# Two stores of rows summed on chip, issued without waiting for the accumulating transfers in DRAM

## Chip, cores and metric

The kernel runs on one core of one Trainium2 chip. The metric is the device time of one execution in microseconds (us). Each core has five engines that work side by side (TensorE, VectorE, ScalarE, GpSimd and SyncE, in the profile PE, DVE, ACT, POOL and SP) and 16 DMA engines, which all of its queues share: SP's queue (q1 in the profile), ACT's (q10) and GpSimd's (q0, whose transfers are made by software).

## What is computed

The input is x of shape (4, 256, 32, 32), that is 4096 tokens of 256 channels. Three blocks follow each other:

```python
x = gamma * attention_along_the_last_axis(x) + x
t = to_tokens(x)
t = t + norm(t) @ W1 + (memory @ norm(t)) @ W2 + bias
u = norm(t)
sel_val, sel_idx = top_k(sigmoid(u @ expert_sel.T), 2)
...
h = relu(einsum('td,edh->teh', u, keys))
out = einsum('teh,te,ehv->tv', h, w, values)
t = t + out
```

Each token goes to 2 of 32 experts, each with 64 hidden values. The last line is what the change concerns: the result of a token is the sum of two rows, one for each of its experts. The row of the first expert also carries the token's own value t.

## The kernel before

The work is cut into 32 tiles of 128 tokens. A first stage computes attention, the memory step, the norm and the routing of each tile, and GpSimd scatters two rows of each token, one for each expert, to a list in DRAM that is sorted by expert. Then comes the expert stage: 20 groups (`GROUPS`) of 4 slots of 128 rows. For each group SP loads the rows, TensorE transposes and multiplies them, VectorE weights the result and adds it (`weighted`, L1161), and GpSimd scatters every row with an indirect transfer to the output (`send_group`, L612 to L620). The tensor `out` has 2N = 8192 rows of 1 KB: the first expert's result of token i goes to row i, the second's to row N + i. Only rows 0 to N - 1 are read by the host in the end, so the second half must be added to the first. This is the drain, which starts when the last scatter has landed, and it does that for two sets of rows in two ways:

- **Rows 0 to 3327** (`IN_PLACE`, L47) are added in DRAM. GpSimd waits for all scatters (L628, L629) and issues four transfers (`SUMS`, L44) from the second half of `out` to the first that add to what they write (L632); each counts the semaphore `stored` up by 16.
- **Rows 3328 to 4095**, the tail (`TAIL_ROWS` = 6, L46), are added on chip. SP loads the tail of the first half (L448), ACT that of the second half (L843), each 768 KB as 128 partitions of 1536 numbers. VectorE adds them in two halves (L1203, `tail_added`), and SP stores the one half (L451) and ACT the other (L846), 384 KB each. Both count up `tail_stored`.

The two sets of rows have no row in common. The engines run independent programs in the order written; a wait holds up the instructions behind it on the same engine alone. In this kernel SP waits for `stored` (L450) ahead of its store, and ACT has a wait for the same value (L845) ahead of its own. At the end SP waits for both stores (L452, `tail_stored` at 32). No other engine waits for `stored` or `tail_stored`. The block ends when all engines are through (L69 in the trace stands for this end of each engine's program).

Of the kernel before, what the change touches and what calls it, by code (L numbers as in the profile page):

```python
# [43 lines left out]
SUMS = 4  # L44
# [21 lines left out]
def attention_moe(nc, x_cm, x_tok, wqk4, bqk4, wvT, bv, gamma, w1, w2, bias, selT, keys, values, out):  # L66
    slots_d = nc.dram_tensor("slot_rows", [NE * CAP + P, ROW], F32, kind="Internal").ap()

    with ExitStack() as ctx:  # L69
# [6 lines left out]
        def sem(name):  # L76
            return ctx.enter_context(nc.semaphore(name))
# [194 lines left out]
        stored = sem("stored")  # L272
# [28 lines left out]
        def tail_rows(r):  # L301

            return out[r * N + IN_PLACE:(r + 1) * N, :].rearrange("(p k) e -> p (k e)", k=TAIL_ROWS)

        def tail_half(i):
            return slice(i * TAIL_ROWS * C // 2, (i + 1) * TAIL_ROWS * C // 2)
# [68 lines left out]
        def _(sp):  # L375
# [71 lines left out]
                sp.wait_ge(y_sent[i], sent_before(GROUPS))  # L447
            sp.dma_start(tail[:, 0], tail_rows(0)).then_inc(ld_tail[0], 16)  # L448
            sp.wait_ge(tail_added, 1)
            sp.wait_ge(stored, 16 * SUMS)  # L450
            sp.dma_start(tail_rows(0)[:, tail_half(0)], tail[:, 0, tail_half(0)]).then_inc(tail_stored, 16)  # L451
            sp.wait_ge(tail_stored, 32)  # L452

        @block.gpsimd
        def _(pool):
# [179 lines left out]
        def _(act):  # L635
# [206 lines left out]
                act.wait_ge(y_sent[i], sent_before(GROUPS))  # L842
            a.dma_start(tail[:, 1], tail_rows(1)).then_inc(ld_tail[1], 16)  # L843
            act.wait_ge(tail_added, 2)
            act.wait_ge(stored, 16 * SUMS)  # L845
            a.dma_start(tail_rows(0)[:, tail_half(1)], tail[:, 0, tail_half(1)]).then_inc(tail_stored, 16)  # L846

        @block.vector
# [685 lines left out]
```

## Time and profile before

| what | us |
|---|---|
| median of 3 runs | 490.43 |
| lowest and highest of them | 489.68, 490.91 |
| span of the profiled execution, first to last instruction | 449.5 |
| median less the span | 40.9 |
| last scatter of the expert stage issued | 420.72 |
| accumulating transfers issued | from 423.45 |
| stores of the tail issued | 445.3 |

The page gives the profiled execution by its span; its own device time is not given, so the 40.9 us around the span are the median of the runs less the span. Times within the profile count from the start of the span. To read it: look for the place of the change at the very end of the timeline, for what SP waits there, and for what the DMA engines do in that time. In the tables by stretch, the DMA share is the mean busy share of the 16 DMA engines; it can come out a little over 1 because a packet's recorded time begins before that of the packet ahead of it has ended.

### The profile page before, as it was taken

Reading aid. Unit: us, or ns where it says so; the run is one execution under the profiler, and the core shown is the slowest. Engines: PE = TensorE matmul, PEld = TensorE weight load, DVE = VectorE, ACT = ScalarE, POOL = GpSimd, SP = SyncE. Lnnn points to the kernel's source line nnn. Section 1 sums busy time; section 2 is a strip of 40 time slices with the busy share of each in tenths; the row PEclk is TensorE's granted clock in tenths of the full one; section 3 lists DMA queues with packets and bytes.
Section 4 is the critical chain, followed back from the end, with each engine's and each line's share of the span. In section 5 each row is a group of like instructions: output and inputs, shape, how many; then the busy total and the mean of one; then the engine's idle time right before and its main releaser. Section 6 shows DMA issues by size and latency. Waiting matters only on the chain.

```text
span 449.5 us, 10462 instructions
## 1 busy us (share of the span) xinstructions
PE 379.7 (84%) x3007; PEld 291.5 (65%) x3007; DVE 334.4 (74%) x1027; ACT 277.4 (62%) x819; POOL 295.9 (66%) x383
## 2 busy tenths in 40 slices
PE   8989999999999999999999998768799969881000
PEld 3756787876787877787878786525687768771000
DVE  1865788986998986898999995883699988894010
ACT  1243577766677775777778785826599879770000
POOL 6334456775777776777788888763667777777700
PEclk9999999999999999999999999968899989898555
DMA  7999310141121111131121111126888665531297
GB/s 207 365 203 190 103 43 25 51 151 37 52 93 49 48 49 50 49 96 49 37 71 49 62 38 71 61 72 199 255 260 249 180 188 175 157 104 40 85 242 186
DMA packets 31321, 52.73 MB, mean 117 GB/s; under 512 B 7036, under 2 KB 24334, under 8 KB 30765
## 3 DMA queue, kind: packets, MB, share of 16 engines
q1 hardware_dynamic: 23104, 29.48, 24.4%
q0 software_dynamic: 7872, 21.40, 15.0%
q10 hardware_dynamic: 288, 1.18, 0.7%
q8 instruction: 25, 0.41, 0.4%
q14 instruction: 32, 0.26, 0.2%
HBM read 31.56 MB, written 25.73 MB: 127 GB/s over the span
## 4 chain that ended last, share of the span: by engine, by line
PE 51%; DVE 19%; issue 9%; POOL 6%; DMA 6%; ACT 3%; DVEq 2%; SPq 1%; ACTq 0%; POOLq 0%
PE bank L1347 21%; PE bank L1309 9%; PE bank L1238 6%; PE bank L1330 4%; DVE rows L1180 3%; DVE vT L1166 3%; PE bank L1337 3%; DMA out<-vT,dest 3%; POOL out L617 3%; DVE vT L862 2%; DVE z_lo L872 2%; DMA xc_or_xin<-out 2%; POOL slot_rows L520 2%; DVE q_s L1149 1%; PE bank L1220 1%
## 5 line engine op out<-in xcount | busy, mean ns | idle before, releaser
L1347 PE MATMUL bank<-vT,prob 128*128 128x256 f32 x512 | 116.0, 380 | 1.7 <-POOL prob L543 1.7
L1347 PEld LDWEIGHTS bank<-vT,prob 128*128 128x128 f32 x512 | 94.9, 190 | 14.1 <-POOL prob L543 2.3
L617 POOL DMA_INDIRECT out<-vT,dest x80 | 79.6, 996 | 28.4 <-issue 14.9
L520 POOL DMA_INDIRECT slot_rows<-rows,slot x64 | 65.0, 1015 | 16.7 <-issue 15.1
L543 POOL TENSOR_TENSOR prob<-prob,ginv 128x1024 f32<-128x1024 f32 x32 | 61.3, 1914 | 21.0 <-DVE ginv L964 21.0
L514 POOL TENSOR_TENSOR rstd<-rstd,half_neg 128x1 f32<-128x1 f32 x64 | 35.9, 561 | 46.9 <-ACT rstd L667 46.5
L726 ACT ACTIVATE prob<-prob 128x1024 f32<-128x1024 f32 x32 | 33.8, 1057 | 19.6 <-DVE prob L932 19.6
L928 DVE TENSOR_REDUCE gmax<-X 128x32 f32<-128x1024 f32 x32 | 39.2, 1224 | 7.9 <-PE X L1272 7.8
L958 DVE TENSOR_REDUCE gsum<-prob 128x32 f32<-128x1024 f32 x32 | 38.7, 1210 | 3.6 <-ACT prob L726 3.5
L932 DVE TENSOR_TENSOR prob<-X,gmax 128x1024 f32<-128x1024 f32 x32 | 39.2, 1224 | 1.1
L1166 DVE SCALAR_TENSOR_TENSOR vT<-bank,wgt,vT 128x256 f32<-128x256 f32 x80 | 33.2, 477 | 6.7 <-PE bank L1485 5.3
L1180 DVE COPY rows<-values_s 64x256 f32 x112 | 34.4, 307 | 3.6 <-issue 2.4
L1238 PE MATMUL bank<-wv,xc_or_xin 128*128 128x256 f32 x128 | 32.6, 384 | 2.4 <-DVE t L880 2.4
L663 ACT ACTIVATE squares<-t,mv 128x256 f32<-128x256 f32 x64 | 31.7, 495 | 2.2 <-DVE t L880 2.1
L862 DVE SCALAR_TENSOR_TENSOR vT<-bank,gam,gbv 128x256 f32<-128x256 f32 x32 | 14.9, 479 | 24.4 <-PE bank L1238 24.3
L822 ACT ACTIVATE k_s<-keys_s 128x128 f32 x112 | 24.7, 306 | 9.4 <-issue 9.3
L1238 PEld LDWEIGHTS bank<-wv,xc_or_xin 128*128 128x128 f32 x128 | 23.5, 189 | 9.1 <-DVE t L880 3.8
L703 ACT ACTIVATE rows<-t,rstd 128x256 f32<-128x256 f32 x32 | 19.2, 599 | 16.0 <-POOL rstd L516 16.0
L800 ACT ACTIVATE prob<-X 128x512 f32<-128x512 f32 x40 | 21.5, 590 | 11.3 <-PE X L1454 11.2
L807 ACT ACTIVATE vT<-xc_or_xin 128x256 f32<-128x256 f32 x48 | 24.8, 593 | 5.1 <-DMA out<-vT,dest 5.1
L1309 PE MATMUL bank<-w_hi,uT_hi 128*128 128x512 f32 x60 | 26.4, 440 | 0.1
L1466 PE MATMUL X<-prob,k_s 128*128 128x256 f32 x96 | 24.4, 400 | 0.7 <-ACT prob L800 0.7
(205 smaller groups left out, 851.6 us busy)
## 6 DMA issues: line engine op xcount, KB each, us to landing
xc_or_xin<-slot_rows SPq DMA_DIRECT2D x32, 130.0 KB
xt<-x_tok SPq DMA_DIRECT2D x32, 128.0 KB, 2.1
values_s<-values SPq DMA_DIRECT2D x2, 2048.0 KB, 28.5
out<-out POOLq DMA_DIRECT2D x4, 832.0 KB, 14.9
xc_or_xin<-x_cm SPq DMA_DIRECT2D x3, 1024.0 KB, 9.2
t<-slot_rows SPq DMA_DIRECT2D x16, 130.0 KB
t<-slot_rows SPq DMA_DIRECT2D x32, 65.0 KB
xc_or_xin<-slot_rows SPq DMA_DIRECT2D x32, 65.0 KB
```

The source lines that it names most:

```text
L514: g.tensor_tensor(rstd[:, t % 2, 1:2], rstd[:, t % 2, 0:1], half_neg[:, :], ALU.pow).then_inc(rstd_done, 1)
L520: g.indirect_dma_start(out=slots_d, out_offset=bass.IndirectOffsetOnAxis(ap=slot[:, t % RB, r:r + 1], axis=0), in_=rows[:, t % RB, r, :], ...
L543: g.tensor_tensor(prob[:, t % 2], prob[:, t % 2], ginv[:, t % 2].unsqueeze(2).to_broadcast([P, WT * KB, W]), ALU.mult).then_inc(prob_done, 1)
L617: g.indirect_dma_start(out=out, out_offset=bass.IndirectOffsetOnAxis(ap=dest[:, n % (2 * NB), k:k + 1], axis=0), in_=yb[:, n % NB, k, :], ...
L928: v.tensor_reduce(gmax[:, s % 2].rearrange("p (w j) -> p w j", w=WT), E.rearrange("p w (j v) -> p w j v", v=W), AX.X, ALU.max).then_inc(ma ...
L932: v.tensor_tensor(prob[:, s % 2].rearrange("p (j w) v -> p w j v", w=WT), E.rearrange("p w (j v) -> p w j v", v=W), gmax[:, s % 2].rearran ...
L958: v.tensor_reduce(gsum[:, s % 2], prob[:, s % 2], AX.X, ALU.add).then_inc(sum_done, 1)
L1166: v.scalar_tensor_tensor(out=yb[:, n % NB, k, :], in0=Y_p[n % 2][k % 2][:, k // 2, :], scalar=wgt[:, n % (2 * NB), k:k + 1], in1=yb[:, n % ...
L1180: done = v.tensor_copy(into, values_s[side, bass.ds(expert[2 * k + r], 1), :].rearrange("p e n -> p (e n)"))
L1238: mm = m.matmul(dst, x, w, start=(i == 0), stop=(i == len(terms) - 1))
L1309: mm = m.matmul(hz_at(t), u[:, t % 2, a, :], w[:, a].rearrange("p s n -> p (s n)"), start=(i == 0), stop=(i == len(terms) - 1))
L1347: mm = m.matmul(av_p, pr[:, j, :], vT[:, b % 2, j, :], start=(j == 0), stop=(j == KB - 1))
```

## The change

The wait for `stored` leaves both places ahead of the stores. SP gets it back behind its wait for `tail_stored`, as the last instruction of its program; ACT has none any more.

```diff
--- before.py
+++ after.py
@@ -447,9 +447,9 @@
                 sp.wait_ge(y_sent[i], sent_before(GROUPS))
             sp.dma_start(tail[:, 0], tail_rows(0)).then_inc(ld_tail[0], 16)
             sp.wait_ge(tail_added, 1)
-            sp.wait_ge(stored, 16 * SUMS)
             sp.dma_start(tail_rows(0)[:, tail_half(0)], tail[:, 0, tail_half(0)]).then_inc(tail_stored, 16)
             sp.wait_ge(tail_stored, 32)
+            sp.wait_ge(stored, 16 * SUMS)
 
         @block.gpsimd
         def _(pool):
@@ -842,7 +842,6 @@
                 act.wait_ge(y_sent[i], sent_before(GROUPS))
             a.dma_start(tail[:, 1], tail_rows(1)).then_inc(ld_tail[1], 16)
             act.wait_ge(tail_added, 2)
-            act.wait_ge(stored, 16 * SUMS)
             a.dma_start(tail_rows(0)[:, tail_half(1)], tail[:, 0, tail_half(1)]).then_inc(tail_stored, 16)
 
         @block.vector
```

No instruction that does work is added, taken out or moved. The waits differ on SP and ACT alone. On SP, at the end of its program (each row is a transfer or the end of the program, in brackets the semaphores it waits for):

```order
 L439 DMA xc_or_xin<-slot_rows 64x260
 L448 DMA xc_or_xin<-out 128x1536 [waits y_sent2,y_sent3,y_sent1,y_sent0]
-L451 DMA out<-xc_or_xin 128x768 [waits stored,tail_added]
-L69 UNCONDITIONAL_BRANCH [waits tail_stored]
+L450 DMA out<-xc_or_xin 128x768 [waits tail_added]
+L69 UNCONDITIONAL_BRANCH [waits stored,tail_stored]
```

The store now waits for the sum alone, and the end of the program for both. On ACT, at the same place:

```order
 L807 ACTIVATE vT<-xc_or_xin 128x256 x3
 L843 DMA xc_or_xin<-out 128x1536 [waits y_sent2,y_sent3,y_sent1,y_sent0]
-L846 DMA out<-xc_or_xin 128x768 [waits stored,tail_added]
+L845 DMA out<-xc_or_xin 128x768 [waits tail_added]
 L69 UNCONDITIONAL_BRANCH
```

Here the wait is gone, and none comes behind it.

## Rows read from the trace of the kernel before

**Rows 1.** page, busy tenths and DMA traffic in 40 slices of 11.2 us

```profile
DMA  7999310141121111131121111126888665531297
GB/s 207 365 203 190 103 43 25 51 151 37 52 93 49 48 49 50 49 96 49 37 71 49 62 38 71 61 72 199 255 260 249 180 188 175 157 104 40 85 242 186
```

**Rows 2.** timeline from 415 us: start us, us, engine, line, transfer

```profile
422.89 0.34 SPq L448 DMA_DIRECT2D xc_or_xin<-out  x1
422.90 0.38 ACTq L843 DMA_DIRECT2D xc_or_xin<-out  x1
423.45 3.55 POOL L632 DMA_DIRECT2D out<-out  x4 [1.75 <-DMA out<-vT,dest]
430.76 1.83 DVE L1203 TENSOR_TENSOR xc_or_xin<-xc_or_xin 128x768 f32<-128x768 f32 x2 [21.27 <-DMA xc_or_xin<-out]
445.31 0.34 SPq L451 DMA_DIRECT2D out<-xc_or_xin  x1
445.33 0.38 ACTq L846 DMA_DIRECT2D out<-xc_or_xin  x1
```

**Rows 3.** waits of the SP queue from 423 us: us, times, longest

```profile
SPq L450 <- DMA out<-out: 22.0, 1, 22.0
SPq L69 <- DMA out<-xc_or_xin: 3.0, 1, 3.0
SPq L69 <- PEq L69: 0.6, 1, 0.6
```

**Rows 4.** source L632, the four accumulating transfers

```profile
DMA to landing us min/median/max: 9.8/14.9/20.1
```

**Rows 5.** windows of 1 us; the last two numbers are DMA share, GB/s

```profile
426.00:427.00 1.00, 0.00 (x0) 0.00 (x0) 0.00 (x0) 0.00 (x0) 1.00 (x2) 0.50 1.02 412
443.00:444.00 1.00, 0.00 (x0) 0.00 (x0) 0.00 (x0) 0.00 (x0) 0.00 (x0) 0.50 1.03 213
444.00:445.00 1.00, 0.00 (x0) 0.00 (x0) 0.00 (x0) 0.00 (x0) 0.00 (x0) 0.50 0.38 73
445.00:446.00 1.00, 0.00 (x0) 0.00 (x0) 0.00 (x0) 0.00 (x0) 0.00 (x0) 0.50 0.00 0
```

**Rows 6.** DMA queues, 428 to 430 us: packets, MB, share of the 16 engines

```profile
q0 software_dynamic: 48, 0.32, 77.3%
q10 hardware_dynamic: 37, 0.17, 21.9%
q1 hardware_dynamic: 26, 0.06, 8.8%
```

**Rows 7.** the same from 431 to 444 us, accumulation alone

```profile
DMA packets 464, 2.77 MB, mean 213 GB/s; under 512 B 48, under 2 KB 48, under 8 KB 464
...
q0 software_dynamic: 464, 2.77, 103.7%
```

**Rows 8.** the same with the issues (KB, us to landing) from 445.5 to 448.5 us, the stores alone

```profile
DMA packets 288, 0.79 MB, mean 262 GB/s; under 512 B 32, under 2 KB 32, under 8 KB 288
...
q10 hardware_dynamic: 144, 0.39, 33.6%
q1 hardware_dynamic: 144, 0.39, 32.7%
...
out<-xc_or_xin SPq DMA_DIRECT2D x1, 384.0 KB, 3.1
out<-xc_or_xin ACTq DMA_DIRECT2D x1, 384.0 KB, 3.3
```

**Rows 9.** windows at the end of the accumulation, same columns

```profile
444.30:444.60 0.30, 0.00 (x0) 0.00 (x0) 0.00 (x0) 0.00 (x0) 0.00 (x0) 0.50 0.16 22
444.60:444.70 0.10, 0.00 (x0) 0.00 (x0) 0.00 (x0) 0.00 (x0) 0.00 (x0) 0.50 0.03 0
444.70:445.30 0.60, 0.00 (x0) 0.00 (x0) 0.00 (x0) 0.00 (x0) 0.00 (x0) 0.50 0.01 0
```

## The prediction

> **What bounds the kernel now.** Only the drain can change, so I read the profile from its end. First the page's busy tenths [rows 1]: in the last three and a half slices TensorE's work is over and the DMA engines are at 9 tenths again; the reader is to see that the end of this kernel is a DMA stage. Then the timeline [rows 2]: the two tail loads are issued at 422.9, the four accumulating transfers from 423.45 on, VectorE adds the tail from 430.76 for 1.83 us, and then no engine does anything until 445.3, when both stores are issued, 12.7 us after the sum was ready. The waits of SP [rows 3] say for what: 22.0 us, up to 445.3, for the accumulation. Its last transfer landed 20.1 us after its issue [rows 4]; issued near 425.2, that is 445.3 too. So the chain of the end is: accumulation landed (445.3), SP issues its store (0.34 us), waits 3.0 us for both stores, which gives 448.65, and then 0.85 us go by until the span's end at 449.5, with 0.6 us of it in the closing barrier [rows 2, 3].
>
> The third view is the one that decides, the DMA share by stretch. From 443 to 444, with the accumulation alone, all 16 engines are taken (share 1.03, 213 GB/s), and the same holds for the 13 us from 431 to 444 (103.7%) [rows 5, 7]. There is no idle DMA time into which the stores could be put before 444.3 or so. Idle are the DMA engines only afterwards: the last packets of the accumulation end by 444.7, SP learns of it 0.6 us later, and from 445 to 446 nothing moves at all [rows 5, 9].
>
> **The change, part by part.**
>
> 1. *The wait ahead of the stores goes.* SP's store can be issued when the first half is added, 430.76 + 0.92 = 431.7, ACT's when the second is, at 432.6 [rows 2]. What leaves the path is the whole stretch from 445.3 to 448.65: 0.34 + 3.0 = **3.34 us**, if `stored` still arrives at 445.3. What is late next is `stored` itself.
>
> 2. *The stores' bytes now stand in the way of the accumulation.* Alone, the two stores took 33.6 + 32.7 = 66.3% of the 16 engines over 3.0 us, which is 1.99 us of every engine, with 256 data packets (288 less 32 small ones), 16 on each engine at 0.12 us [rows 8]. By bytes it is the same: 0.79 MB in 1.99 us are 397 GB/s. How much of it delays the accumulation the trace doesn't show directly, so I bound it. From below: nothing, if a store's packet could be moved beside an accumulating one, since the rate while accumulating is only 213 GB/s against the 412 of the loads alone [rows 5]. From above: I take twice the price, 4.0 us, as for engines that lose as much again at every turn between queues. The nearest row is the stretch from 428 to 430, in which the last tail loads ran beside the accumulation [rows 6]: 0.32 MB of accumulation are worth 0.32/0.213 = 1.50 us at its own rate, 0.17 + 0.06 = 0.23 MB of loads at 412 GB/s 0.56 us, together 2.06 us of work in 2 us. So the queues took turns and hid 3% of it. I take the full 1.99 us: `stored` is seen at 445.3 + 2.0 = 447.3.
>
>  What the slow rate means is a question on which the Trainium skill bears. The row: 213 GB/s of bytes written, 0.54 of the stores' rate [rows 7, 8]. The rule (Collectives: The Full Stack, "The bandwidth ceiling: the fold count and why AG ≠ RS ≠ AR"): an add in a DMA is slower not by its arithmetic but because it must read two sources over one read ring, which halves the rate. The trace's ratio of 0.54 agrees with it. By that rule the reading side is full, and a store, which must read too, is delayed in full, as I take it; if it were the adder that is slow, the sum would lean to the lower bound and save 3.3 us.
>
> 3. *In which order the packets go doesn't matter.* The accumulation has 32 data packets a microsecond, 2 on an engine, so 0.5 us each (464 less 48 small ones in 13 us) [rows 7]. One of each queue in turn makes 8 rounds of 0.5 + 2 x 0.12 us, 6 us, and the stores would land before 440. If they were served last of all, they would end with the accumulation at 444.6 + 2.0. The engines' work is the same sum, so the last landing stays near 447.3.
>
> 4. *The wait at SP's end.* Nothing is queued behind it but the closing barrier. ACT is through after its issue; VectorE, GpSimd and TensorE wait for neither semaphore. SP's other wait, for the stores, is over by then or ends with it. The 0.85 us behind the last landing stay.
>
> The sum: the span ends at 445.3 + 2.0 + 0.85 = 448.15 in place of 449.5, **1.35 us less** (3.34 - 1.99). Against the median, 40.9 us above the span, it is 490.43 - 1.35 = **489.1 us**, or 0.27%. A measurement of this kernel can tell about 0.3%, here 1.47 us, from no change, and its three runs spread over 1.2 us; the forecast lies just inside that bound.
>
> **The rivals.**
>
> *Part of the stores is hidden.* The loads of [rows 6] read DRAM as the accumulation does; the stores read the chip's own memory, which the accumulation never touches, and could fill gaps better than they did. If a third of the 1.99 us is hidden, the saving is 3.34 - 1.33 = 2.0 us, and the time 488.4; if all is, 487.1. For it: the shares above 1, which show packets overlapping. Against: 1.037 is the accumulation's share even alone [rows 7], so what overlap there is it has already. The Trainium skill would put the time near there too (DMA: Bandwidth & Descriptors, "Anatomy of one DMA — SWDGE (gpsimd) path": a fixed 2.0 us a transfer, mostly the confirmation of the last write, plus bytes over 436 GB/s): the fixed part would leave the path, 2.0 us, for 488.4. For the stores here the rows show 3.34 us less 1.99 us of moving, a fixed part of 1.35 us.
>
> *The turns cost something.* If the accumulating packets run longer beside the stores, say 0.1 us in each of 8 rounds, 0.8 us of the gain is lost, and the time is 489.9. [Rows 6] speak against it, though for loads only.
>
> *Slower: reads and writes collide in DRAM.* The loads only read DRAM; the stores write it, in the middle of an accumulation that reads and writes it as well. All gain is lost when the delay reaches 3.34 us, 1.35 more than the packets' own time: 0.17 us for each of the 8 accumulating packets of an engine that run beside a store, 0.50 to 0.67. To be slower by over 0.3% it takes 2.8 us more, 0.35 us each, for 491.9. Nothing in the trace looks like it: the rate is 213 GB/s in every stretch [rows 5, 7], whatever is being written.
>
> *The stores go early in name only.* Should their packets be held back until the accumulation is done, they would land 2.6 us after 444.6, near 447.2, and `stored` no later than 445.3: again about 1.4 us saved. The order of the landings would differ, the time hardly.
>
> **How the numbers follow.** The forecast, with a saving of 1.1 to 1.6 us however the packets are ordered, gets 0.62; a measurement puts about a third of that beyond 0.3% (0.20) and the rest within (0.42). Part hidden 0.24, all of it faster. Turns that cost something 0.11, within 0.3%. Slower 0.03. That makes 0.44 faster, 0.53 no difference, 0.03 slower. The range goes down to 488.0, a delay of 0.9 us by the stores, and up to 490.2, where the turns take nearly all of the gain; the ends beyond, 487.1 and 491.9, are left out.
>
> **What would show it.** Right: stores issued at 431.7 and 432.6 and landed near 440; from 432 to 439 a mixed rate above 213 GB/s with all engines taken; the last accumulating transfer landed about 2 us later than now, near 447.3; SP's last long wait for that transfer, and 0.85 us behind it. Wrong: a landing at 445.3 to 446.5 (stores hidden), or beyond 448.2 (turns or DRAM). If the drain is as I say and the time is not, it lies outside the span.

## The result, and the profile after

The change makes the kernel slower: a median of 491.47 us against 489.61 us, in 14 runs each, a ratio of 1.0044 with a 95% interval of 1.0026 to 1.0062, that is some 2.1 us by the ratio. The forecast was 489.1 us, 1.35 us less, with 0.03 for slower by over 0.3%.

One number of the prediction has to be put right first. Every later profile names the time of its own execution, and it is 1.7 to 2.2 us above its span: here 490.86 us for a span of 489.1 us. So the first profile of the kernel before, with its span of 449.5 us, was of an execution of some 451 us, 35 us below the fastest (486.24 us) of 43 timed runs of that kernel, in this comparison and the first one below (481.85 us is the lowest in the later ones); the "40.9 us around the span" are the difference of two unlike executions. The unchanged kernel profiled again (b_again) has a span of 488.9 us. The 40 us lie in the expert stage, as the rows of its scatters show, in the first trace and in b_again (durations in ns, first and last start in us):

```profile
L617 POOL DMA_INDIRECT out<-vT,dest x80: 978/981/1102, 314.9 to 420.7; - x80
```

```profile
L617 POOL DMA_INDIRECT out<-vT,dest x80: 978/980/988, 316.0 to 460.4; - x80
```

Its first scatter comes at nearly the same time, its last one 40 us later; why that one execution was faster stays open. The drain behind it is the same in both within 0.3 us, and traces are compared below by what follows the issue of the accumulation.

The end of the timeline after the change (start us, us, engine, line, transfer), against [rows 2]:

```profile
460.25 0.34 SPq L448 DMA_DIRECT2D xc_or_xin<-out  x1
460.26 0.38 ACTq L843 DMA_DIRECT2D xc_or_xin<-out  x1
460.82 3.55 POOL L632 DMA_DIRECT2D out<-out  x4 [1.75 <-DMA out<-vT,dest]
467.92 1.83 DVE L1202 TENSOR_TENSOR xc_or_xin<-xc_or_xin 128x768 f32<-128x768 f32 x2 [14.85 <-DMA xc_or_xin<-out]
468.90 0.34 SPq L450 DMA_DIRECT2D out<-xc_or_xin  x1
469.77 0.35 ACTq L845 DMA_DIRECT2D out<-xc_or_xin  x1
```

The waits of the SP queue behind that point (us, times, longest), against [rows 3]:

```profile
SPq L452 <- DMA out<-out: 15.7, 1, 15.7
SPq L450 <- DVE xc_or_xin L1202: 8.3, 1, 8.3
SPq L447 <- DMA out<-vT,dest: 5.1, 1, 5.1
SPq L69 <- PEq L69: 3.9, 1, 3.9
```

The issues' times to landing (KB, us), against [rows 4, 8]:

```profile
out<-out POOLq DMA_DIRECT2D x4, 832.0 KB, 16.7
...
out<-xc_or_xin SPq DMA_DIRECT2D x1, 384.0 KB, 10.2
out<-xc_or_xin ACTq DMA_DIRECT2D x1, 384.0 KB, 10.7
```

The stores do what the change says: issued at 468.9 and 469.8 and landed some 10 us later, at 479.1 and 480.5, they are through 4 us before the accumulation lands at 484.9. The 15.7 us at L452 begin when SP has issued its store, so they hold both waits, the one for the stores and the one for `stored`; the second ends last. The last row of the waits is the one that matters: in the closing barrier SP now waits 3.9 us where it waited 0.6 [rows 3]. The name of its releaser (PE's queue) is no help: TensorE's own end of program is over at 451.3 us, 34 us before SP comes to the barrier. Who is late there is shown by the rows of L69, which stands for the end of each engine's program (engine, operation, durations in ns, start). In the kernel before:

```profile
L69 PEldq DRAIN  x1: 2023/2023/2023, 405.7 to 405.7; - x1
L69 POOLq DRAIN  x1: 24492/24492/24492, 424.7 to 424.7; - x1
L69 DVEq DRAIN  x1: 1803/1803/1803, 430.8 to 430.8; - x1
L69 ACTq DRAIN  x1: 152/152/152, 445.7 to 445.7; - x1
...
L69 SPq DRAIN  x1: 7/7/7, 448.8 to 448.8; - x1
```

and after the change:

```profile
L69 PEldq DRAIN  x1: 3808/3808/3808, 447.5 to 447.5; - x1
L69 POOLq DRAIN  x1: 26777/26777/26777, 462.1 to 462.1; - x1
L69 DVEq DRAIN  x1: 1805/1805/1805, 468.0 to 468.0; - x1
L69 ACTq DRAIN  x1: 162/162/162, 470.2 to 470.2; - x1
...
L69 SPq DRAIN  x1: 7/7/7, 485.1 to 485.1; - x1
```

GpSimd ends its program with a DRAIN that starts as its last transfer is issued, so it looked like nothing but waiting for the accumulation. But it ends at 424.7 + 24.5 = 449.2 before, when the accumulation landed at 445.3, and at 462.1 + 26.8 = 488.9 after, when it landed at 484.9: **3.9 to 4.0 us behind the last landing, both times**. In the kernel before the stores (3.34 us) fitted under that. By this reading they were never on the path, and the change only puts the accumulation off; the runs below test it.

### The profile page after: what moved, and what is told of

It reads as the page before. It is cut to its first block, busy times and chain, and to the rows that moved or that the text cites. A ratio compares the mean times of both kernels' runs of the same rounds, so it can differ in the third digit from the quotient of the medians.

```text
span 489.1 us, 10458 instructions
## 1 busy us (share of the span) xinstructions
PE 393.3 (80%) x3004; PEld 300.4 (61%) x3007; DVE 337.0 (69%) x1027; ACT 279.4 (57%) x819; POOL 295.1 (60%) x383
## 4 chain that ended last, share of the span: by engine, by line
PE 48%; issue 13%; DVE 12%; SPq 11%; POOL 5%; DMA 3%; ACT 2%; another core or an unknown queue 1%; DVEq 1%; ACTq 0%; POOLq 0%
PE bank L1346 19%; SPq L439 7%; PE bank L1308 7%; PE bank L1237 5%; PE bank L1329 4%; PE bank L1336 3%; DVE vT L861 2%; SPq L436 2%; DVE z_lo L871 2%; POOL out L617 2%; DMA xc_or_xin<-out 2%; POOL slot_rows L520 1%; PE X L1465 1%; PE bank L1219 1%; PE bank L1320 1%
## 5 line engine op out<-in xcount | busy, mean ns | idle before, releaser
L617 POOL DMA_INDIRECT out<-vT,dest x80 | 78.6, 982 | 66.1 <-DVE vT L1165 44.3
L800 ACT ACTIVATE prob<-X 128x512 f32<-128x512 f32 x40 | 22.3, 590 | 50.7 <-remote 24.2
L1179 DVE COPY rows<-values_s 64x256 f32 x112 | 37.6, 335 | 3.2 <-issue 1.9
L1453 PE MATMUL X<-ident,xc_or_xin 128*128 128x128 f32 x96 | 16.9, 328 | 21.7 <-DMA xc_or_xin<-slot_rows 12.2
L861 DVE SCALAR_TENSOR_TENSOR vT<-bank,gam,gbv 128x256 f32<-128x256 f32 x32 | 14.9, 479 | 24.3 <-PE bank L1237 24.3
L822 ACT ACTIVATE k_s<-keys_s 128x128 f32 x112 | 24.6, 301 | 11.2 <-issue 10.5
L1453 PEld LDWEIGHTS X<-ident,xc_or_xin 128*128 128x128 f32 x96 | 13.2, 168 | 26.0 <-DMA xc_or_xin<-slot_rows 14.3
L1465 PE MATMUL X<-prob,k_s 128*128 128x256 f32 x96 | 26.1, 420 | 2.6 <-issue 1.9
L1148 DVE TENSOR_SCALAR q_s<-X 64x256 f32<-64x256 f32 x24 | 10.1, 422 | 25.4 <-remote 17.9
```

Of the source, the lines that this page charges most:

```text
L617: g.indirect_dma_start(out=out, out_offset=bass.IndirectOffsetOnAxis(ap=dest[:, n % (2 * NB), k:k + 1], axis=0), in_=yb[:, n % NB, k, :], ...
L1179: done = v.tensor_copy(into, values_s[side, bass.ds(expert[2 * k + r], 1), :].rearrange("p e n -> p (e n)"))
```

## Experiments

All but b_no_sums, which has no accumulation, are compared by the same four times (us): how long after its own issue the last accumulating transfer landed, how far behind that landing the DRAIN ended, what SP waited in the closing barrier, and E, from the issue of the first accumulating transfer (L632) to the end of the span.

| kernel | landing after issue | DRAIN's end behind landing | SP waits in barrier | E | ratio to before (95%) |
|---|---|---|---|---|---|
| before, first trace | 20.1 | 3.9 | 0.6 | 26.05 | 1 |
| b_again | 19.9 | 4.0 | 0.6 | 25.8 | |
| the change | 22.3 | 4.0 | 3.9 | 28.3 | 1.0044 (1.0026 to 1.0062) |
| b_no_stores | 20.0 | 4.0 | 3.9 | 26.0 | 1.001 (0.9975 to 1.0045) |
| half_early | 21.2 | 3.9 | 1.6 | 27.15 | 1.001 (0.9982 to 1.0038) |
| a_double | 24.3 | 3.9 | 3.9 | 30.2 | 1.0075 (1.004 to 1.011) |
| b_double | 20.0 | 4.0 | 0.2 | 27.5 | |
| b_pool_waits | 20.4 | 8.1 | 4.7 | 30.6 | 1.0063 (1.0035 to 1.0091) |
| b_sums1 | 21.8 | 3.9 | 0.5 | 25.9 | 0.9984 (0.9952 to 1.0016) |
| b_sums8 | 18.5 | 4.1 | 0.7 | 26.6 | |
| b_no_drain | 20.0 | none | 0.2 | 25.7 | 1.0007 (0.998 to 1.0035) |
| a_no_drain | 22.8 | none | 0.2 | 25.1 | 0.9978 (0.9948 to 1.0008) |
| a_no_drain_2 | 22.2 | none | 0.2 | 24.45 | 0.9966 (0.9942 to 0.9989) |

**The kernel before, again.**

> The kernel before, unchanged, for a second trace. My theory now: the program ends with the DRAIN at the end of GpSimd's program (L69), which starts when the last accumulating transfer is issued and ends 3.9 to 4.0 us after that transfer has landed, while the two stores take only 3.3 us of it; so SP's last wait, for the closing barrier, is again 0.5 to 0.7 us. The rival, on which the prediction rested: the stores end last, and 0.85 us behind them is fixed. The first trace's span of 449.5 us lies far below the 487 to 491 us of the other runs; if the expert stage of that execution was an exception, this span is near 488.

Its L69 rows and SP's waits:

```profile
L69 POOLq DRAIN  x1: 24317/24317/24317, 464.4 to 464.4; - x1
```

```profile
SPq L450 <- DMA out<-out: 21.9, 1, 21.9
...
SPq L69 <- DMA out<-xc_or_xin: 3.0, 1, 3.0
...
SPq L69 <- PEq L69: 0.6, 1, 0.6
```

All of it as expected: landing at 464.8 + 19.9 = 484.7, DRAIN until 488.7, span 488.9, one run of 490.71 us.

**The stores left out.** This is the run that decides between the two theories of the end.

```diff
-            sp.dma_start(tail_rows(0)[:, tail_half(0)], tail[:, 0, tail_half(0)]).then_inc(tail_stored, 16)
-            sp.wait_ge(tail_stored, 32)
...
-            a.dma_start(tail_rows(0)[:, tail_half(1)], tail[:, 0, tail_half(1)]).then_inc(tail_stored, 16)
```

> The kernel before without the two stores of the tail and the wait for them (rows 3328 to 4095 of the output are not stored). Theory of GpSimd's drain: the stores were hidden under it, so the time stays that of the kernel before (ratio 1.000, within 0.1%), and SP waits some 4 us in the closing barrier. Rival (stores on the path): 3.3 us less, ratio 0.993.

```profile
SPq L450 <- DMA out<-out: 22.0, 1, 22.0
SPq L69 <- PEq L69: 3.9, 1, 3.9
```

The ratio is 1.001, and its interval ends at 0.9975, above the 0.993 of the rival. Both stores can be taken out of the kernel without making it faster; E is 26.0 us, where it was 25.8 and 26.05 with them. SP is done 3.9 us early, as after the change. The stores were hidden.

**The early stores doubled.**

```diff
 sp.dma_start(tail_rows(0)[:, tail_half(0)], tail[:, 0, tail_half(0)]).then_inc(tail_stored, 16)
+sp.dma_start(tail_rows(1)[:, tail_half(0)], tail[:, 0, tail_half(0)]).then_inc(tail_stored, 16)
-sp.wait_ge(tail_stored, 32)
+sp.wait_ge(tail_stored, 64)
...
 a.dma_start(tail_rows(0)[:, tail_half(1)], tail[:, 0, tail_half(1)]).then_inc(tail_stored, 16)
+a.dma_start(tail_rows(1)[:, tail_half(1)], tail[:, 0, tail_half(1)]).then_inc(tail_stored, 16)
```

> The changed kernel with each store of the tail issued twice, the second time to the matching rows of the second half of the output, which nobody reads after that. Theory (the stores' 2.0 us on the DMA engines put off the accumulation, whose landing plus 4 us is the end): another 2.0 us, ratio to the kernel before 1.0085, that is 4 us in all; the last accumulating transfer lands 26 us after its issue in place of 22.3. Rival (the loss comes from where the wait stands, or from the stores' writes as such): the ratio stays 1.0044.

```profile
DMA to landing us min/median/max: 9.9/17.0/24.3
```

```profile
L69 POOLq DRAIN  x1: 28728/28728/28728, 463.5 to 463.5; - x1
```

The landing moves by another 2.0 us, to 24.3, the DRAIN with it, and E from 28.3 to 30.2. The 26 us named before the run were too many: 22.3 + 2.0 are the 24.3 measured. The ratio of 1.0075 is a little under the 1.0085 named, well within its interval, and the rival's 1.0044 lies at its lower edge; the verdict rests on the trace.

**Half of the change.** Against the kernel before:

```diff
 sp.wait_ge(tail_added, 1)
-sp.wait_ge(stored, 16 * SUMS)
 sp.dma_start(tail_rows(0)[:, tail_half(0)], tail[:, 0, tail_half(0)]).then_inc(tail_stored, 16)
 sp.wait_ge(tail_stored, 32)
+sp.wait_ge(stored, 16 * SUMS)
```

> One part of the change alone: SP's store goes early (its wait for the accumulation stands at the end of SP's program), ACT's keeps its wait. Theory (each early store takes its own 1.0 us of the DMA engines from the accumulation, and the end is the last landing plus 4 us): half the loss, 1.0 us, ratio about 1.002; the last accumulating transfer lands 21.1 us after its issue, between 20.0 and 22.3. Rival (it is the wait's place in a program, not the bytes, that costs): the whole 1.0044, or nothing.

```profile
DMA to landing us min/median/max: 9.9/15.7/21.2
```

By the trace it is half: a delay of 21.2, between 20.0 and 22.3, and E 27.15, between 25.8 to 26.05 and 28.3. The runs alone don't tell: 0.9982 to 1.0038 holds no change, half the loss, and nearly the whole.

**The stores doubled behind the accumulation**, in the kernel before, with the same added lines as a_double.

> The kernel before with each store of the tail issued twice behind the accumulation. Theory: the stores need 5.3 to 5.7 us behind the last landing, the DRAIN 3.9, so now the stores end last and SP's wait in the closing barrier falls from 3.9 (no stores) and 0.6 (one store) to about that of a barrier with nobody late (under 0.6 us); the DRAIN still ends 3.9 us behind the landing. Rival: the DRAIN moves with the stores and ends behind them again.

```profile
SPq L69 <- DMA out<-xc_or_xin: 4.5, 1, 4.5
...
SPq L69 <- PEq L69: 0.2, 1, 0.2
```

```profile
L69 POOLq DRAIN  x1: 24419/24419/24419, 457.7 to 457.7; - x1
...
L69 SPq COMPARE_BRANCH  x1: 38/38/38, 483.5 to 483.5; - x1
```

The last accumulating transfer lands at 458.1 + 20.0 = 478.1, SP issues its first store at 478.2, and the DRAIN ends at 457.7 + 24.4 = 482.1, 4.0 us behind it as ever. Now the stores take longer than that: SP is through at 483.5, the span ends at 483.9, and SP waits 0.2 us in the barrier, as in the runs below without a DRAIN: that much the barrier takes where nobody is late. The DRAIN was over 1.4 us before the stores landed, so its end does not wait for transfers of SP and ACT. The cover of the stores is thus 4 us wide, and one set of stores used 3.34 of it.

**What the DRAIN does.** Four runs. In the first GpSimd waits for the accumulation itself, so that its DRAIN starts with nothing of GpSimd's own under way:

```diff
 g.dma_start(sums_d[0][c], sums_d[1][c], accum_op=ALU.add,
             max_dma_last_dim=4 * SUM_ROWS * C).then_inc(stored, 16)
+pool.wait_ge(stored, 16 * SUMS)
```

> The kernel before, with GpSimd itself waiting for the accumulation at the end of its program, so that its DRAIN starts only then. If the DRAIN has 4 us of its own to do once the queue is empty: same time as before, a DRAIN of some 4 us. If it spends its time in watching transfers under way and has nothing left once they have landed: a DRAIN under 0.5 us, the stores end last, and the time is 0.5 us less than before (ratio 0.999). If it does work from its start that only then ends: longer than before.

```profile
L69 POOLq DRAIN  x1: 7915/7915/7915, 483.5 to 483.5; - x1
```

The DRAIN takes 7.9 us of its own and the kernel gets slower by 0.6%. Both easy pictures of it fall: it isn't idle watching, and it isn't a fixed 4 us at the end either. That some 4 of the 7.9 us can be done while the transfers run, and the rest only behind them, would fit both numbers; no run shows it.

The second leaves out the four accumulating transfers and the two waits for `stored` (its output is then the first expert's part alone for rows 0 to 3327).

> The kernel before without the accumulating transfers and the waits for them (rows 0 to 3327 keep the first expert's part alone). GpSimd's DRAIN then starts when all scatters have landed. If its own work is a fixed one, or belongs to the 144 and more indirect transfers before it: 7.9 us, as where it started after the accumulation. If it belongs to the accumulating transfers alone: under 0.5 us.

```profile
L69 POOLq DRAIN  x1: 7589/7589/7589, 460.6 to 460.6; - x1
```

7.6 us, though no accumulating transfer had been issued. So the price does not come with the accumulating transfers. Here it costs nothing: it ends at 468.2, and the stores end last, at 471.3.

The third and fourth issue the same sum as one transfer or as eight (`SUMS = 1`, `SUMS = 8`).

> The kernel before with one accumulating transfer of 3328 rows in place of four of 832. If the part of the DRAIN behind the last landing (3.95 us) is a cost per transfer: about 1 us of it is left, the stores end last (0.6 us in the closing barrier), and the time is some 0.6 us less plus 1 to 2 us for less issuing, ratio 0.995 to 0.999. If it is fixed, or goes by bytes or packets: 3.9 us again, the ratio within 0.2% of 1.

> The kernel before with eight accumulating transfers of 416 rows. If the DRAIN costs by the transfer: some 8 us behind the last landing; if it is fixed or goes by bytes: 3.9 us again. SP's wait in the closing barrier is that less 3.3 us.

```profile
L69 POOLq DRAIN  x1: 25681/25681/25681, 461.9 to 461.9; - x1
```

```profile
L69 POOLq DRAIN  x1: 23379/23379/23379, 463.4 to 463.4; - x1
```

With one transfer the landing is at 461.9 + 21.8 = 483.7 and the DRAIN ends at 487.6; with eight at 464.1 + 18.5 = 482.6 and 486.8. That is 3.9 and 4.1 us behind the landing, so it doesn't go by the number of transfers. What the 7.6 to 7.9 us are spent on stays open: a cost that grows with the 148 indirect transfers that GpSimd issued before would look the same in all of these runs, and that wasn't tried.

**The DRAIN taken away.** Every transfer of GpSimd in this kernel is waited for by semaphore anyway, and the block can be closed without the DRAIN; the engines then meet in a barrier of semaphores alone.

```diff
-        block = ctx.enter_context(nc.Block())
+        block = ctx.enter_context(nc.Block(no_gpsimd_drain=True))
```

> The changed kernel with the DRAIN taken off the end of GpSimd's program (every transfer of GpSimd is waited for by its semaphore in any case). Theory: the end is now the last landing of the accumulation plus some 0.3 us; it comes 2.2 us later than in the kernel before but 3.9 us of DRAIN behind it are gone: 1.7 us less than the kernel before, ratio 0.9965, and 3.6 to 3.9 us less than the changed kernel. SP's wait in the closing barrier is under 0.7 us. Rival (the DRAIN only fills a time that something else sets): the changed kernel's time, 1.0044.

> The kernel before with the DRAIN taken off the end of GpSimd's program. Theory: the stores now end last, 3.3 us behind the landing, where the DRAIN ended at 3.9: 0.6 us less than the kernel before at most, ratio 0.999. Against this kernel, a_no_drain should be 1.1 us faster, which is what the prediction meant the change to bring. Rival: both without DRAIN the same, or the kernel before the faster of the two.

With the change (a_no_drain), the last landing, SP's end and the span's end lie together. Its waits, and the issues' times to landing:

```profile
SPq L452 <- DMA out<-out: 16.1, 1, 16.1
...
SPq L69 <- PEq L69: 0.2, 1, 0.2
```

```profile
out<-out POOLq DMA_DIRECT2D x4, 832.0 KB, 17.2
```

and without the change (b_no_drain):

```profile
SPq L69 <- DMA out<-xc_or_xin: 3.0, 1, 3.0
...
SPq L69 <- PEq L69: 0.2, 1, 0.2
```

```profile
out<-out POOLq DMA_DIRECT2D x4, 832.0 KB, 14.8
```

SP's wait in the barrier is 0.2 us in both. Without the DRAIN the kernel before gains next to nothing, as the stores take its place: E is 25.7 in place of 25.8 to 26.05, where up to 0.6 us were expected, and the ratio is 1.0007. The change, which cost 2.2 to 2.5 us of E with the DRAIN, now saves 0.55: 25.1 against 25.7. Its direction has turned in the traces, but 1.1 us were expected of that difference; here the early stores put the landing off by 2.8 us, not 2.2. In the main for the same reason the changed kernel without the DRAIN is 0.7 to 0.9 us below the kernel before, where 1.7 were expected. The runs don't tell a_no_drain and b_no_drain apart (0.9978 and 1.0007, with intervals that overlap).

Change and missing DRAIN together looked like a version better than both kernels, so it was run a second time.

> The same kernel as a_no_drain once more, in runs of its own, since its interval of 0.9948 to 1.0008 does not tell it from the kernel before. By its trace it should be 0.7 to 0.9 us less, from the issue of the accumulation to the end: ratio 0.998 to 0.9985. Rival: the drain at GpSimd's end stands for work that has to be done somewhere, and the ratio is 1 or more.

The ratio was 0.9966, from 0.9942 to 0.9989: faster than the kernel before (medians of 484.58 against 486.58 us). In this trace the landing comes 22.2 us after the issue and E is 24.45, which is 1.2 us less than b_no_drain's 25.7 and 1.4 to 1.6 less than the kernel before (0.997), where 0.7 to 0.9 were expected from the trace of a_no_drain. So in the two traces the change without the DRAIN saves 0.55 and 1.2 us. The two are of one kernel and 0.65 us apart, and they are set against a single trace of b_no_drain: that the change saves there is shown in its direction by the traces alone, its size is not.

## Why the prediction was wrong, by its own steps

- *What bounds the kernel.* The DMA engines were full until 444.3 and the end of the kernel is a DMA stage: right. The chain behind the landing was the step that failed: "accumulation landed (445.3), SP issues its store (0.34 us), waits 3.0 us for both stores, which gives 448.65, and then 0.85 us go by". Two things end behind the landing, the stores by 3.34 us and GpSimd's DRAIN by 3.9, and the later one was not seen. The 0.6 us in the closing barrier were quoted as a part of a fixed 0.85 us, when they said that SP, with its stores landed, was waiting for somebody later. The trace of the kernel before had the answer in the rows of L69, which were not read. The prediction's own signs of being right came true but for the last: early stores, a landing some 2 us later, and then not 0.85 us behind it but 4.2. Its way out, that a wrong time would lie outside the span, pointed away from the place.
- *Part 1, "what leaves the path is the whole stretch", 3.34 us*: nothing left the path: with no stores at all E is 26.0 us, as with them (b_no_stores).
- *Part 2, the stores' 1.99 us of all DMA engines delay the accumulation in full*: right, and somewhat small. The landing came 22.3 us after the issue in place of 19.9 to 20.1, a delay of 2.2 to 2.4 us. The surplus is seen in the stretch in which the stores ran beside the accumulation:

```profile
q0 software_dynamic: 182, 1.10, 74.9%
q1 hardware_dynamic: 144, 0.39, 14.5%
q10 hardware_dynamic: 130, 0.39, 13.1%
```

  1.10 MB at 213 GB/s are 5.16 us and 0.78 MB at the stores' 397 GB/s 1.96 us, together 7.1 us of work in 7.5 us: some 0.4 us more than the work. The engines were not idle in it, as the shares add to 102.5%, where the accumulation alone gives 103.7%. Rather the packets took longer beside each other: by its recorded time an accumulating data packet took 0.545 us (74.9% of 7.5 us on 16 engines, for 1.10 MB in some 165 packets of 6.7 KB), where it takes 0.519 alone (103.7% of 13 us, for 416) [rows 7].

  The rival "the turns cost something" thus was true, with 0.03 us a packet in place of its 0.1: 0.2 to 0.4 us of delay in all (0.8 in a_no_drain), where the loads had shown none [rows 6]. The Trainium skill (DMA: Bandwidth & Descriptors, "Issuing engines are not separate DMA queues") says that transfers run on the same 16 engines whoever issues them, and that several issuers save only the time of issuing. The delays of 1.1 to 1.3 us for one early store, 2.1 to 2.9 for two and 4.2 to 4.4 for four, against 19.9 to 20.1 with none, agree with it. The 2.0 us fixed part that the prediction set beside its rival of hidden stores is the Trainium skill's fit for transfers issued by GpSimd; these stores are issued by SP and ACT, and nothing of them was hidden.
- *Part 3, the order doesn't matter*: right. The stores landed 10.2 and 10.7 us after their issue, later than turns of 6 us give, and `stored` came 4 us later still.
- *Part 4, "the 0.85 us behind the last landing stay"*: it is 4.2 us behind the landing of the accumulation (3.9 to 4.0 of DRAIN, the rest barrier), before and after. That GpSimd waits for neither semaphore was true and beside the point: its DRAIN ends by the landing of its own transfers all the same.
- *The slower rival* had a wrong mechanism (reads and writes that collide in DRAM). The slower outcome had a simple price that its chance of 0.03 ignored: 1.99 us of stores moved from a place where they are free.

With the DRAIN in the chain the same sum gives the result: nothing saved, 1.99 to 2.4 us lost, 0.4 to 0.5%; measured 0.44%. The chain itself is the kernel's own: where the DRAIN is gone (a_no_drain against b_no_drain), the traces have the change saving time, as was argued, by 0.55 and 1.2 us in place of 1.35; the timed runs leave it open.

## What to carry to other kernels

A wait in a closing barrier that is longer than the barrier itself takes (0.2 us in this kernel, with nobody late) says that another engine ends later than the one you watch, even at 0.6 us: go through every engine's last instruction, and if in doubt leave the supposed last work out and see whether the time falls. Work placed behind a full DMA stage can be free where an engine has something of its own to finish there, and moving it into the full stage then costs its whole transfer time, here 2.0 us and a little more.

## What the hardware showed that was not expected

GpSimd's closing DRAIN takes 7.6 to 7.9 us with none of its transfers under way, and ends 3.9 to 4.1 us behind the landing of the last one where it starts earlier. That held for one, four or eight transfers, and with or without other traffic. Closing the program without it took 3.1 and 3.8 us off the changed kernel by the traces (E from 28.3 to 25.1 and 24.45). What the DRAIN does in its time no run shows.
